# One GpSimd add of two token blocks per state instead of two, in a fused attention, scan and expert kernel

## The reference

```python
x = x + attention(layernorm(x))            # L0
x = x + fp8_like_gemm(layernorm(x))        # L0
x = x + mamba(layernorm(x))                # L1, with its own inner norm; adds its residual again
x = x + moe(layernorm(x))                  # L1, 8 experts, 2 of them for each token, and a shared one
# inside mamba, for 512 channels d and 16 states s:
h[t, d, s] = exp(delta[t, d] * A[d, s]) * h[t-1, d, s] + delta[t, d] * u[t, d] * B[t, s]
y[t, d]    = sum over s of h[t, d, s] * C[t, s]
```

## Time and profile before

| | |
|---|---|
| Time, 3 runs | 3400.44 us median (3392.41 to 3403.95) |
| Profiled execution, its own time | 3394.05 us |
| its span, first to last instruction | 3392.3 us |
| busy over the span: PE, DVE, ACT, POOL | 84%, 76%, 61%, 76% |
| mean granted TensorE clock | 0.926 |
| POOL adds of 128x512 at line 858 | 480, mean 1272 ns |

### The profile page before, as it was taken

One profiled execution on the slowest core, in us unless ns is written; L12 is line 12 of the kernel. 1 busy time (PEld: TensorE's weight loads), 2 busy tenths in 40 slices (PEclk: granted clock), 3 DMA queues, 4 the chain that ended last, 5 costly groups with the idle time before them and its releaser, 6 DMA issues. The chain is left out here.

```text
span 3392.3 us, 46798 instructions
## 1 busy us (share of the span) xinstructions
PE 2848.8 (84%) x12696; PEld 1875.0 (55%) x12697; DVE 2573.3 (76%) x4153; ACT 2063.8 (61%) x3770; POOL 2594.0 (76%) x2474
## 2 busy tenths in 40 slices
PE   4686979797979797978888888888887779999998
PEld 2444555555555554555555555554545447777776
DVE  3598989898999989898989898989897842222222
ACT  3577676676767676767767676766665513444443
POOL 1499898989898898989898989898989923444444
PEclk7897989898989898989999999999988879999999
DMA  2001111111111111111110101010112313333333
GB/s 74 23 33 32 34 44 35 42 37 41 38 38 41 38 39 38 45 35 44 32 51 28 50 29 51 29 48 30 43 34 79 104 52 58 62 62 62 62 62 53
DMA packets 113898, 155.38 MB, mean 46 GB/s; under 512 B 15472, under 2 KB 73264, under 8 KB 113712
## 3 DMA queue, kind: packets, MB, share of 16 engines
q1 hardware_dynamic: 77344, 109.32, 10.4%
q0 software_dynamic: 25728, 34.75, 6.2%
q10 hardware_dynamic: 10640, 9.09, 0.8%
HBM read 107.36 MB, written 45.76 MB: 45 GB/s over the span
## 5 line engine op out<-in xcount | busy, mean ns | idle before, releaser
L872 POOL TENSOR_TENSOR dbu<-du,bbc 128x512 f32<-128x512 f32 x1024 | 1296.2, 1281 | 107.1 <-DVE h L1438 100.8
L1438 DVE TENSOR_TENSOR_SCAN h<-bank,dbu 128x512 f32<-128x512 f32 x1024 | 1226.1, 1211 | 159.7 <-ACT bank L1079 98.1
L1079 ACT ACTIVATE bank<-region,amat 128x512 f32<-128x512 f32 x1024 | 703.5, 691 | 320.8 <-DVE h L1438 308.0
L665 PE MATMUL bank<-ident,h 128*128 128x128 f32 x4096 | 626.4, 289 | 264.1 <-DVE acc L1428 234.3
L665 PEld LDWEIGHTS bank<-ident,h 128*128 128x128 f32 x4096 | 497.8, 148 | 548.6 <-DVE acc L1428 218.1
L858 POOL TENSOR_TENSOR acc<-acc,hTc 128x512 f32<-128x512 f32 x480 | 610.2, 1272 | 96.3 <-ACT hTc L1063 94.2
L1605 POOL DMA_INDIRECT out<-ye,ids x136 | 213.3, 1569 | 347.5 <-DMA out<-ye,ids 309.2
L1063 ACT ACTIVATE hTc<-bank,cT 128x512 f32<-128x512 f32 x480 | 327.2, 682 | 249.1 <-PE bank L665 243.8
L1428 DVE SCALAR_TENSOR_TENSOR acc<-bank,cT,acc 128x512 f32<-128x512 f32 x544 | 394.3, 729 | 37.3 <-PE bank L665 31.4
L619 PE MATMUL bank<-x4T,w_su 128*128 128x512 f32 (+1 forms) x768 | 395.9, 619 | 10.7 <-DVE score L1298 10.7
L1641 DVE SCALAR_TENSOR_TENSOR gg<-gt,bank 128x352 f32<-128x352 f32 x136 | 70.9, 521 | 382.5 <-ACT gt L1575 382.5
(11 more groups left out here) (204 smaller groups left out, 4297.4 us busy)
## 6 DMA issues: line engine op xcount, KB each, us to landing
bbc<-b_scratch SPq DMA_DIRECT2D x256, 256.0 KB, 3.1
xe<-slots_in SPq DMA_DIRECT2D x136, 129.0 KB
region<-in_x SPq DMA_DIRECT2D x16, 512.0 KB, 3.8
out<-x ACTq DMA_DIRECT2D x16, 512.0 KB, 3.0
region<-in_e_gu SPq DMA_DIRECT2D x8, 704.0 KB, 5.5
out<-ye,ids POOLq DMA_INDIRECT x136
slots_in<-dbu SPq DMA_DIRECT2D x16, 129.0 KB, 3.0
slots_in<-x,pos POOLq DMA_INDIRECT x128
```

What stands on the lines that cost most here:

```text
L665: last = tr(scan[f"hT{s}.{t}"][:, m * P:(m + 1) * P], h[:, s % 2, m, t * P:(t + 1) * P], ident[:, :])
L872: g.tensor_tensor(dbu[:, n % 4, :], du[:, m, :], bbc[:, (b * NS + s) % NROW, :], ALU.mult).then_inc(S("dbu_ready"), 1)
L1079: f(db(n)[:, :], delta[:, 1 - par, m, :], ACT.Exp, scale=amat[:, m, s:s + 1]).then_inc(S("da_ready"), 1)
L1438: v.tensor_tensor_scan(h[:, s % 2, m, :], db(n)[:, :], dbu[:, n % 4, :], 0.0, ALU.mult, ALU.add)\
```

## The change

POOL adds blocks 1 and 3 of a state in one operation of 128x2x512, at the place where block 3 was added: `acc` blocks 1 and 3 (a stride of two blocks) plus both slots of `hTc`. `acc_added` now counts 15 for each sequence instead of 30. ACT, before it scales block 1 or 3 of state s, waits until the add of state s-1 is done; who reads `acc` waits for the same count.

```diff
-                   ... acc_added=len(POOLED), y3_ready=MC,
+                   ... acc_added=len(POOLED) // 2, y3_ready=MC,
@@ acc_before
-                done(eng, "acc_added", b, POOLED.index((s - 1, t)))
+                done(eng, "acc_added", b, s - 1)
@@ POOL
-                    if (s, t) not in POOLED:
+                    if t < TT - 1 or s == NS - 1:
                         return
-                    k = POOLED.index((s, t))
-                    done(pool, "scaled", b, k)
-                    acc_before(pool, b, s, t)
-                    g.tensor_tensor(acc[:, t, :], acc[:, t, :], hTc[:, k % 2, :], ALU.add).then_inc(S("acc_added"), 1)
+                    done(pool, "scaled", b, POOLED.index((s, t)))
+                    for odd in (1, 3):
+                        acc_before(pool, b, s, odd)
+                    odds = acc[:, :, :].rearrange("p (k two) d -> p k two d", two=2)[:, :, 1, :]
+                    g.tensor_tensor(odds, odds, hTc[:, :, :], ALU.add).then_inc(S("acc_added"), 1)
@@ ACT
                     scan.filled(act, f"hT{s}.{t}", b)
-                    before(act, "acc_added", b, k - 1)
+                    before(act, "acc_added", b, s)
                     f(hTc[:, k % 2, :], scan[f"hT{s}.{t}"][:, :], ACT.Copy, scale=cT[:, par, t, s:s + 1]).then_inc(S("scaled"), 1)
```

More of the change, by code:

```diff
@@ L272, in layers @@
                    b_stored=1, cT_ready=1, da_ready=UNITS, dbu_ready=UNITS,
-                   scan_done=UNITS, acc_init=TT, acc_ready=len(KEPT), scaled=len(POOLED), acc_added=len(POOLED), y3_ready=MC,
+                   scan_done=UNITS, acc_init=TT, acc_ready=len(KEPT), scaled=len(POOLED), acc_added=len(POOLED) // 2, y3_ready=MC,
                    x3_ready=2, x4_ready=1, x4T_ready=DC, lexp_ready=1, sg_ready=1, tag_ready=1, pos_ready=1, tok_set=1, weight_set=1,
```

## The result

| | before | after |
|---|---|---|
| median of 4 runs, us | 3402.19 (3392.41 to 3408.47) | 3433.34 (3430.22 to 3435.71) |
| ratio | 1 | 1.0083, 95% interval 1.0064 to 1.0102 |
| profiled span, us | 3392.3 | 3433.1 |
| mean granted clock | 0.926 | 0.921 |

The change costs 28 us by the ratio, 31 by the medians. The profile of before was a quick execution (a second one, in the experiments, spans 3400.6), so the 40.8 us between the two traces overstate it by some 8.

A forecast was written before the change was run, and what follows sets the result against it. DVE's scans, waiting mostly for ACT's exp, set the pace. The profiled 3394.05 - 5 (turns 14 and 15) + 18 (turn starts) = 3407; the +13 put on median 3400.44 and rounded down gave 3412 us, range 3385 to 3434.

The forecast's parts named there:

- rival 2: Mid-turn, in states like 8: ACT's block 1 waits for the previous state's add; 15 us on top, 3428; chance 0.07.
- The operation: POOL's merged add: 2.36 us against 2544 ns for two, 0.19 us less per state, 45 us of POOL time.
- Turns 14 and 15, -5 us: Last two turns, where scans wait 11.1 us for POOL: its saved time counts, -5 us, bounds 0 and 11.1.
- ACT's wait in mid-turn, 0: Block 1 scaled 0.53 us late in one or two states a turn, mostly hidden: nothing counted, 15 us if in full.
- The end of a turn: ACT scales block 14.1 0.66 us late, POOL's next `du` comes 1.76 us later, scan 6 1.5 us later.
- with the same 0.07 us: Turn's end: state 13's add starts 0.07 us after block 13.3 is scaled, running 1434.33 to 1436.69.
- Who carries the delay: Turn's start: POOL, with 0.26 us of slack, passes its lateness through the norm chain and ACT to scan 6.
- Line 948 (now 949) idles for line 805: Turn's start, a sign of the forecast being right: ACT's line 948 idles for POOL's line 805.
- A turn's price, 1.3 us: Late start costs between 0 and 2.75 us a turn, 1.3 taken; over 14 boundaries +18 us, bounds 0 and 38.
- The sample of turns 3 and 4: Compared with turn 8: turn 4's late start went with +2.75 us; turn 3's late scan 6 was nearly all made good.
- The port, 0 with bounds of -7 and +11: Turn's start: a longer POOL add can hold a two-input DVE operation 1.1 us longer; 0 taken, bounds -7 and +11 us.
- Rival 3: DVE held at the port: a tiny two-input operation meets the long add; +11 us alone, 3411; chance 0.05.
- Rivals 4 and 5: Start delay made good, POOL's saving idle, about 3399, chance 0.33; or POOL's saving shortens scans' waits, 3384, chance 0.17.

The follow-up runs named there:

- the run of thirteen states: Kernel before with the add merged in states 0 to 12 only, the last two states added apart as before: 3406.48 us, 1.0017.
- the run with states 7 and 10 alone: Kernel before with the add merged only in states 7 and 10 of each turn: 3418.62 us, 1.0056.
- states 2 to 4: Kernel before with the add merged only in states 2, 3 and 4: 3389.01 us, 0.9969.
- the late place: Kernel before with two separate adds moved to where the merged one stands, ACT waiting only for its own slot's add: 3411.2 us, 1.0033.
- the pair wait: Two separate adds where the merged one stands, ACT waiting for both adds of the state before: 3422.38 us, 1.0074.
- all but 13 and 14: Kernel before with the add merged in states 0 to 12, states 13 and 14 added apart: 3406.48 us, 1.0017.
- state 14 alone: Kernel before with the add merged only in state 14 of each turn: 3423.34 us, 1.0078.
- 13 alone: Kernel before with the add merged only in state 13 of each turn: 3422.58 us, 1.0074.
- 3 and 4: Kernel before with the add merged only in states 3 and 4: 3391.97 us, 0.9982.
- pair wait alone: Kernel before, adds in their old places, only ACT's wait changed to both adds of the state before: 3411.71 us, 1.0038.

## Why the prediction was half right

The forecast was 3412 us, slower, with the turn's end as the cause. The direction holds, and the turn's end is one of the places; the size was +12, and it is +28 to +31. That 3433.34 lies inside the range, 0.7 us below its upper end, is luck: that end was set for rival 2, a wait of ACT in mid-turn, and holds at the port took the space. By its steps:

- *The operation*: 2.36 us expected, 2359 ns measured, 240 times. Right by the group (610.2 to 566.3 us). POOL's busy time, though, fell by 36.0 us (2594.0 to 2558.0), 0.15 a pair and not 0.19: a record here overlaps the next one by some 0.04 us (1626.50 is 0.04 before 1624.19 + 2.35), and the page's busy time counts an overlap once. That is the other price in the prediction, 0.14 us, by the rule of the Trainium skill (Perfetto Trace Analysis, GPSIMD Engine Instruction) to compare starts; the page of after agrees with it.
- *Turns 14 and 15, -5 us*: wrong. The scans' wait for POOL did fall, from 11.1 to 7.8 us, but turn 14 became 6.2 us longer: the product there takes 3.5 us, and its start is late like any other. The term looked at one wait and not at the turn.

```profile
DVE h L1439 <- POOL dbu L873: 7.8, 6, 2.4
```

- *ACT's wait in mid-turn, 0*: the waits came, 0.57 and 0.42 us a turn at blocks 8.1 and 11.1, near the 0.53 of the estimate. That they are hidden is compatible with the run of thirteen states (1.0017) and was not shown by itself: the run with states 7 and 10 alone cost 0.56%.
- *The end of a turn*: the step "with the same 0.07 us" failed. The prediction's own rows spoke against it: the add of 13.3 began at 1435.22, 0.96 us after its block was scaled at 1434.26, since POOL was busy. With the change it is still in the last of three `dbu`, and reaches the add of state 13 0.71 us after the scaling. ACT is 1.34 us late instead of 0.66, the first `du` comes 3.87 us after the last scan's start (1626.50 - 1622.63) instead of the forecast 3.3 and the earlier 1.62: +2.25 us, not +1.76.
- *Who carries the delay*: the sum followed POOL alone, through the norm chain. Scan 0 is late already, which the forecast didn't have, by DVE's wait for PE (1.07 us, from matmuls at the lower clock) and by the hold (1.04 us). POOL still waits 0.26 us for DVE's statistics in ten of the thirteen turns, where I had said that it no longer would: both are late together. In turns 5 and 6, where scan 0 comes at 9.16 and 9.15 us, it waits for nothing, as forecast.

```profile
1639.66 0.20 POOL L776 TENSOR_TENSOR ve<-mv,eps 128x4 f32<-128x4 f32 x1 [0.26 <-DVE mv L1158]
...
1643.73 0.20 POOL L805 TENSOR_TENSOR b<-shift,r 128x4 f32<-128x4 f32 x1
```

- *Line 948 (now 949) idles for line 805*: in turn 5 alone, 0.63 us. In turn 9 ACT went from an exp straight into it, at 1644.14.
- *A turn's price, 1.3 us*: the turns of before were 163.8, those of after 165.4 to 168.5. The mean over turns 1 to 13 grew by 2.45 us (31.9 / 13), near the upper bound of 2.75, but this is not the price of a late start alone: it holds the product's 19.0 us as well. With states 2 to 4 merged scan 6 was 1.15 us late and the turn 163.85 us, so a late start can also cost nothing. The sample of turns 3 and 4 mixed two things, too: at 14 to 16 us into turn 3 and at 15 to 16.4 us into turn 4 TensorE was granted 0.50, in turn 8, the one they were held against, 1.00.
- *The port, 0 with bounds of -7 and +11*: the mis-sized term. Its parts are larger than the bounds and of both signs: +21 us between scans 32 and 44, about +10 at line 1220, -26 between 16 and 32. The 1.1 us that I took as a hold's price is the add's extra length over a `dbu` (2.36 - 1.28), which is right only for an operation that was held before as well. The product was nearly free before (0.29 to 0.32 us) and met the add in the same instant in nine turns of thirteen, for the full 2.24 us. Rival 3 was right in its mechanism, and its sign (lines 1233 and 1319 longer) was wrong: in sum just those became shorter (38.3 to 32.8 us, 18.5 to 4.7).
- *Rivals 4 and 5*: excluded as what happened. Rival 5's outcome, a faster kernel, appears with three states merged, at 0.9969, though not by the mechanism that it named: the scans' waits for POOL are 34.7 us there against 32.0.

What the runs settle: the late place and the pair wait each cost something, in a ladder of 3400, 3411 and 3422 us, and the double length takes it to 3433 by the medians and the traces, though its ratio's interval overlaps that of the rung below. Keeping the product clear of the add takes most of this last rung away. What they don't: a price for each that holds on its own, since one state merged costs as much as two or fifteen, and how much of the loss at a turn's start is TensorE's lower clock there.

The Trainium skill (SBUF — State Buffer, SBUF: two separate sides) says that whichever operation starts first has the shared port pair for its whole length and the other blocks fully. The length agrees with the trace, by the 2.45 us of a product beside a 2.36 us add; who goes first needs care where POOL's operations follow each other without a pause, as the last section shows.

## What to carry to other kernels

Joining two operations of a producer also joins their hand-overs: look at who waited for the first half alone, and what stands behind that waiter. Where DVE and POOL both run two-input operations, a change of POOL's pattern moves every later meeting of theirs; list the small DVE instructions whose mean is several times their minimum, before and after, beside the waits. Where an engine waits longer for TensorE, look at the durations of the matmuls and the granted clock there, before the delay is put down to whoever feeds it. And try an edit of a periodic program in parts, since a part of it may gain (states 2 to 4: 0.9969) where the whole loses (1.0083).

## What the runs showed of the hardware

**Recorded starts don't say who gets in between two POOL operations.** In the changed kernel the product's recorded start is ahead of the add's in turns 1 to 13, by 0.01 to 0.04 us. Ahead by 0.009 to 0.018 us it is held for 2.45 us in seven turns. At 0.04 us it is free in two, and between 0.02 and 0.03 it goes both ways: twice free, twice held. In all but 13 and 14, with 0.05 to 0.08 us, it was free 13 times of 13; in before, 0.15 to 0.18 us ahead, it took 0.29 to 0.32 us. But by the record the product never came to an idle port in these turns: the `dbu` ahead of the add ends 0.07 to 0.24 us after the product's start. It comes as one POOL operation hands over to the next, and either gets in between or waits for the whole next one. The lead is no threshold either: in turn 14 it was held for 2.68 to 2.70 us at 0.11 to 0.14 us ahead (state 14 alone, 13 alone, 3 and 4), and free, with 0.21 to 0.25 us, at 0.08 to 0.13 us ahead (states 2 to 4, pair wait alone, and both traces of before).

**A one-input operation is stretched too.** The 128x4 copy of line 1316 takes 418 ns as the median before and 163 ns after. It stands directly ahead of line 1319, which is held in the same turns. That it is the port which stretches it was not tested.
